# Attention scores on Trainium2: one head in each half of the array's rows, the row maxima added by a second product

## The reference

```
B, S, H, d_k = 4, 1024, 16, 16
Q, K, V = to_heads(split(x @ W_qkv.T)); Q, K = apply_rope(Q), apply_rope(K)
scores = einsum('bhqd,bhkd->bhqk', Q, K) / sqrt(d_k)
scores = where(causal, scores, -inf)
attn = softmax(scores, axis=-1)
out = einsum('bhqk,bhkd->bhqd', attn, V)
```

## Time and profile before

| | us |
|---|---|
| median of 3 runs | 1749.88 |
| lowest and highest | 1743.73, 1751.45 |
| profiled execution | 1757.38 |
| its span | 1755.3 |
| PE busy in the span | 1537.1 (88%) |
| DVE busy | 1001.3 (57%) |
| ACT busy | 734.5 (42%) |
| POOL busy | 573.0 (33%) |

### The profile page before, as it was taken

The page is one execution under the profiler, slowest core; times in us unless marked ns, Lnnn a source line. Parts: engine busy times, 40 slices in busy tenths (PEclk is TensorE's granted clock), DMA queues, the critical chain, the costliest instruction groups (busy, mean ns, idle before and its releaser), DMA issues. The chain is left out here.

```text
span 1755.3 us, 31129 instructions
## 1 busy us (share of the span) xinstructions
PE 1537.1 (88%) x9903; PEld 1148.9 (65%) x9903; DVE 1001.3 (57%) x3394; ACT 734.5 (42%) x1537; POOL 573.0 (33%) x1009
## 2 busy tenths in 40 slices
PE   6999999972999999588698999999999577579978
PEld 3677777752999998344375666666665466468857
DVE  3344555441323232488697888888885456445548
ACT  3444444420222222233245777767777222234410
POOL 3123333323000000677433223223223254535520
PEclk9999999985999999799699999999999788689989
DMA  7001111114777775688869667676660555445536
GB/s 218 1 25 49 49 49 49 37 49 141 207 215 214 209 210 156 184 266 266 224 96 202 93 92 116 92 115 92 92 92 32 175 184 164 129 129 157 157 125 209
DMA packets 170062, 235.21 MB, mean 134 GB/s; under 512 B 25040, under 2 KB 121936, under 8 KB 169776
## 3 DMA queue, kind: packets, MB, share of 16 engines
q1 hardware_dynamic: 134128, 171.55, 42.3%
q0 software_dynamic: 13008, 35.57, 6.1%
q10 hardware_dynamic: 22768, 26.11, 4.7%
HBM read 147.90 MB, written 84.98 MB: 133 GB/s over the span
## 5 line engine op out<-in xcount | busy, mean ns | idle before, releaser
L1983 ACT ACTIVATE t_probs<-t_ps_st 128x512 f32<-128x512 f32 x576 | 313.1, 596 | 134.5 <-PE t_ps_st L2037 125.1
L1964 DVE CUSTOM_DVE_ANT_0 t_seen<-t_ps_s,t_later 128x512 bf16<-128x512 f32 (+3 forms) x512 | 285.7, 587 | 23.3 <-PE t_ps_s L2023 21.3
L2037 PE MATMUL t_ps_st<-t_qs,t_ks 128*128 128x512 f32 (+3 forms) x768 | 244.2, 367 | 6.5 <-ACT t_probs L1983 5.4
L2023 PE MATMUL t_ps_s<-t_ks,t_qs 96*128 96x512 f32 (+3 forms) x768 | 249.1, 364 | 0.6 <-ACT t_neg_max L1976 0.5
L1936 POOL TENSOR_SCALAR_AFFINE_SELECT t_probs<-t_probs 128x128 f32<-128x128 f32 x512 | 137.2, 300 | 313.9 <-ACT t_probs L1983 312.2
L2037 PEld LDWEIGHTS t_ps_st<-t_qs,t_ks 128*128 128x128 f32 x768 | 137.7, 190 | 80.6 <-ACT t_probs L1983 43.4
L1964 DVE CUSTOM_DVE_ANT_0 t_seen<-t_ps_s,t_later,t_first_max 128x512 bf16<-128x512 f32 (+3 forms) x256 | 140.6, 549 | 50.9 <-PE t_ps_s L2023 50.7
L1524 POOL DMA_INDIRECT d_ye<-outputs_dram,r_pos_all x64 | 64.2, 1003 | 303.3 <-POOLq L1304 285.5
L2053 PE MATMUL t_ps_o<-t_probs,t_vs 128*17 128x256 f32 (+1 forms) x2560 | 155.7, 362 | 0.5 <-issue 0.5
L2023 PEld LDWEIGHTS t_ps_s<-t_ks,t_qs 96*128 96x128 f32 x768 | 139.6, 191 | 18.4 <-DVE t_first_max L1964 1.8
L1345 PE MATMUL m_ps_h<-m_xt,m_w_t 128*128 128x128 f32 x1136 | 140.9, 278 | 0.0
(11 more groups left out here) (329 smaller groups left out, 2711.1 us busy)
## 6 DMA issues: line engine op xcount, KB each, us to landing
m_w_t<-in_w_dram SPq DMA_DIRECT2D x71, 512.0 KB, 4.1
t_qs<-qkt_dram SPq DMA_DIRECT2D x124, 128.0 KB, 5.8
t_ks<-qkt_dram SPq DMA_DIRECT2D x124, 128.0 KB, 5.6
m_x_t<-gathered_dram SPq DMA_DIRECT2D x79, 128.5 KB
m_x_t<-gathered_dram SPq DMA_DIRECT2D x71, 128.0 KB, 3.8
outputs_dram<-m_y ACTq DMA_DIRECT2D x71, 128.0 KB, 4.0
qkt_dram<-d_hi ACTq DMA_DIRECT2D x32, 256.0 KB
qkt_dram<-d_lo SPq DMA_DIRECT2D x32, 256.0 KB
```

The source lines that it names most:

```text
L1964: nc.vector.tensor_tensor_reduce(out=seen[:, (NP * p + x) % (RS + 1), 0:keys], in0=bank_of(p, x)[:, 0:keys], in1=masks, scale=1.0, scalar= ...
L1983: nc.scalar.activation(probs[:, p % 2, i // NST, base:base + STC], ps_st[(NX * p + i) % RT][:], ACT.Exp, scale=HD ** -0.5).then_inc(exp_re ...
L2023: nc.tensor.matmul(bank_of(p, x)[:, 0:keys], q[0:MAX_ROW, head, qc * P:(qc + 1) * P], k[0:MAX_ROW, head, k0:k0 + keys], start=True, stop=T ...
L2037: last = nc.tensor.matmul(ps_st[(NX * p + i) % RT][:, col:col + width], k[:, head, kc * P:(kc + 1) * P], q[:, head, q0:q0 + width], start= ...
```

## The change

Head 0 of a pair now lies in partitions 0 to 63 and head 1 in 64 to 127 of tiles half as wide (`[P, SEQ]`). The same bytes are loaded, still by eight DMAs a pair; a broadcast in the source repeats the part of k. A score matmul takes the 64 rows of its head (`half`), and pieces alternate between the heads, one bank each.

The maxima have tiles of their own: `maxima` (two, in turn), row 0 for head 0 and row 64 for head 1, the rest zero, and `first_ones`, whose rows 0 and 64 are one and the rest zero. For each turned product there is a second one that adds it to the same bank. Within a chunk the order is: first product of head 0, of head 1, second product of head 0, of head 1. SP writes the maxima by two DMAs in place of one.

A step is now twice as long: 9 a pair, with the same chunk of both heads, two or four pieces, and averages at steps 0, 2, 4, 5 and 7. `LAG` is 14 of these steps. The transpose stays in step 2, while the chunks of the earlier pair start at step 5, three long steps later; before it was step 9, seven half as long ones later. The negation comes on ACT behind the exponentials of the same step. Three banks for the turned chunks stay. The masks on POOL and the exponentials go by turns through the heads.

```diff
-    rows = hl * 2 * DM + which * DM + (p % PAIRS) * 2 * HD
-    eng.dma_start(dst[part * HD:(part + 1) * HD].bitcast(FP32),
-                  qkt_dram[rows:rows + 2 * HD, bass.ts(p // PAIRS, SEQ)].rearrange("(h d) t -> d h t", h=2)).then_inc(loaded, 16)
+KS = 4 * HD
 
 
 def load_heads(eng, p, q, k, qkt_dram, loaded):
-    for part in range(4):
-        load_head_rows(eng, p, q, 0, part, part % 2, qkt_dram, loaded)
-        load_head_rows(eng, p, k, 1, part, part // 2, qkt_dram, loaded)
+    rows = qkt_dram.rearrange("(l w n d) t -> l w n d t", l=2, w=2, d=HD)
+    cols = bass.ts(p // PAIRS, SEQ)
+    for h in range(2):
+        head = (p % PAIRS) * 2 + h
+        for part in range(2):
+            half = slice(h * KS + 2 * part * HD, h * KS + 2 * (part + 1) * HD)
+            eng.dma_start(q[half].bitcast(FP32), rows[:, 0, head, :, cols]).then_inc(loaded, 16)
+            eng.dma_start(k[half].bitcast(FP32), rows[part:part + 1, 1, head, :, cols].broadcast_to([2, HD, SEQ])).then_inc(loaded, 16)
...
-    MAX_ROW = 96
     RT, RS = 3, 4
-    ks = [k_first] + [sb(f"t_ks{i}", [P, 2, SEQ], FP32R) for i in range(1, RINGQ)]
-    qs = [q_first] + [sb(f"t_qs{i}", [P, 2, SEQ], FP32R) for i in range(1, RINGQ)]
+    ks = [k_first] + [sb(f"t_ks{i}", [P, SEQ], FP32R) for i in range(1, RINGQ)]
+    qs = [q_first] + [sb(f"t_qs{i}", [P, SEQ], FP32R) for i in range(1, RINGQ)]
+    maxima = [sb(f"t_maxima{i}", [P, SEQ], FP32R) for i in range(2)]
+    first_ones = sb("t_first_ones", [P, P], FP32R)
...
-    units = [[u for i in range(NC) for u in ((0, NC - 1 - i), (1, i))], [u for i in range(NC) for u in ((0, i), (1, NC - 1 - i))]]
+    wides = [[NC - 1 - i for i in range(HALF)], [HALF + i for i in range(HALF)]]
     row_pieces = []
-    for each in units:
+    for each in wides:
         mine = []
-        for a, b in zip(each[0::2], each[1::2]):
-            (wh, wq), (nh, nq) = (a, b) if a[1] >= HALF else (b, a)
-            mine += [(wh, wq, 0, STC), (nh, nq, 0, (nq + 1) * P), (wh, wq, STC, (wq + 1) * P - STC)]
+        for wide in each:
+            narrow = NC - 1 - wide
+            for qc, k0, keys in ((wide, 0, STC), (narrow, 0, (narrow + 1) * P), (wide, STC, (wide + 1) * P - STC)):
+                mine += [(head, qc, k0, keys) for head in range(2)]
...
-    upto = [(i + 1) * NP // NX for i in range(NX)]
-    avg_at = {1: (0, 1), 5: (2, 3), 9: (4, 5), 12: (6, 7), 16: (8, 9)}
-    LAG = 27
-    LAST = LAG + (pairs + 1) * NX
+    upto = [2 * ((i + 1) * NP // 2 // NST) for i in range(NST)]
+    avg_at = {0: (0, 1), 2: (2, 3), 4: (4, 5), 5: (6, 7), 7: (8, 9)}
+    LAG = 14
+    LAST = LAG + (pairs + 1) * NST
...
     for p in range(pairs + 1):
-        for i in range(NX):
+        for i in range(NST):
...
             def row(p):
-                s = p % RINGQ
-                if p < RINGQ:
-                    sp.wait_ge(rows_filled, 2 * p + 1)
+                if p == 0:
+                    sp.wait_ge(rows_filled, 5)
+                wait(sp, st_done, NX * (p - 1))
                 sp.wait_ge(neg_ready, p + 1)
-                sp.dma_start(qs[s][MAX_ROW:MAX_ROW + 1].bitcast(FP32).rearrange("o h (c q) -> o (h c) q", c=NC),
-                             neg_max[:, p % 2, :].bitcast(FP32)).then_inc(row_loaded[s], 16)
+                for h in range(2):
+                    sp.dma_start(maxima[p % 2][h * KS:h * KS + 1].bitcast(FP32).rearrange("o (c q) -> o c q", c=NC),
+                                 neg_max[h * NC:(h + 1) * NC, p % 2, :].bitcast(FP32)).then_inc(row_loaded[p % 2], 16)
...
+            nc.gpsimd.memset(first_ones[:].bitcast(FP32), 0.0).then_inc(rows_filled, 1)
+            for m in maxima:
+                nc.gpsimd.memset(m[:].bitcast(FP32), 0.0).then_inc(rows_filled, 1)
...
+            pool.wait_ge(rows_filled, 3)
+            for h in range(2):
+                nc.gpsimd.memset(first_ones[h * KS:h * KS + 1].bitcast(FP32), 1.0).then_inc(rows_filled, 1)
+                pool.wait_ge(rows_filled, 4 + h)
...
-                        dve.wait_ge(piece_ready, NP * p + x - 1)
+                        dve.wait_ge(piece_ready, NP * p + x - 3)
...
             for step in range(LAST):
-                p, i = divmod(step, NX)
-                q, j = divmod(step - LAG, NX)
-                if step == 4 * NX:
+                p, i = divmod(step, NST)
+                q, j = divmod(step - LAG, NST)
+                if step == 4 * NST:
                     fetch(act)
                 if live(q):
-                    exponentials(q, j)
-                if i == 3 and live(p - 1):
+                    exponentials(q, 2 * j)
+                    exponentials(q, 2 * j + 1)
+                if i == TURN and live(p - 1):
                     negate(p - 1)
-                if j == NX - 2 and live(q - 1):
+                if j == NST - 1 and live(q - 1):
                     take_out(q - 1)
...
@@ -2017,10 +2017,9 @@
                 q, k = qs[p % RINGQ], ks[p % RINGQ]
                 if x == 0:
                     pe.wait_ge(qk_loaded[p % RINGQ], 128 * (p // RINGQ + 1))
...
                 bank_free(p, x)
-                nc.tensor.matmul(bank_of(p, x)[:, 0:keys], q[0:MAX_ROW, head, qc * P:(qc + 1) * P], k[0:MAX_ROW, head, k0:k0 + keys],
+                half = slice(head * KS, (head + 1) * KS)
+                nc.tensor.matmul(bank_of(p, x)[:, 0:keys], q[half, qc * P:(qc + 1) * P], k[half, k0:k0 + keys],
                                  start=True, stop=True).then_inc(s_done, 1)
...
-            def chunk(p, i):
-                q, k, head = qs[p % RINGQ], ks[p % RINGQ], i // NST
-                if i == 0:
-                    pe.wait_ge(row_loaded[p % RINGQ], 16 * (p // RINGQ + 1))
-                wait(pe, exp_ready, NX * p + i - RT + 1)
-                for kc, q0, col, width in chunks[i % NST]:
-                    last = nc.tensor.matmul(ps_st[(NX * p + i) % RT][:, col:col + width], k[:, head, kc * P:(kc + 1) * P], q[:, head, q0:q0 + width],
-                                            start=True, stop=True)
-                last.then_inc(st_done, 1)
+            def chunk(p, n):
+                q, k = qs[p % RINGQ], ks[p % RINGQ]
+                if n == 0:
+                    pe.wait_ge(row_loaded[p % 2], 32 * (p // 2 + 1))
+                for kc, q0, col, width in chunks[n]:
+                    for head in range(2):
+                        at, half = NX * p + 2 * n + head, slice(head * KS, (head + 1) * KS)
+                        if col == 0:
+                            wait(pe, exp_ready, at - RT + 1)
+                        nc.tensor.matmul(ps_st[at % RT][:, col:col + width], k[half, kc * P:(kc + 1) * P], q[half, q0:q0 + width],
+                                         start=True, stop=False, skip_group_check=True)
+                    for head in range(2):
+                        at, half = NX * p + 2 * n + head, slice(head * KS, (head + 1) * KS)
+                        last = nc.tensor.matmul(ps_st[at % RT][:, col:col + width], first_ones[half], maxima[p % 2][half, q0:q0 + width],
+                                                start=False, stop=True, skip_group_check=True)
+                        if col + width == STC:
+                            last.then_inc(st_done, 1)
...
             for step in range(LAST):
-                p, i = divmod(step, NX)
-                q, j = divmod(step - LAG, NX)
+                p, i = divmod(step, NST)
+                q, j = divmod(step - LAG, NST)
                 if live(q):
                     chunk(q, j)
                 elif step < LAG:
-                    keep_busy(i, 2 * P)
+                    keep_busy(2 * i, 2 * P)
+                    keep_busy(2 * i + 1, 2 * P)
```

More of the change, by code:

```diff
@@ L1754, in attention @@
     VR = HD + 1
-    KS = 4 * HD
     STC = 4 * P
@@ L1826, in attention @@
     rows_filled, later_zeroed, ones_filled = sem("t_rows_filled"), sem("t_later_zeroed"), sem("t_ones_filled")
+    row_loaded = [sem(f"t_row_loaded{s}") for s in range(2)]
     filled, set_up = sem("t_filled"), sem("t_set_up")
     qk_loaded = [first_loaded] + [sem(f"t_qk_loaded{s}") for s in range(1, RINGQ)]
-    row_loaded = [sem(f"t_row_loaded{s}") for s in range(RINGQ)]
     stored = [sem(f"t_stored{s}") for s in range(2)]
@@ L1916, in _ @@
             pool.wait_ge(set_up, 1)
-            for p in range(1, RINGQ):
-                zero_rows(p)
-                nc.gpsimd.memset(ks[p][KS:P].bitcast(FP32), 1.0).then_inc(rows_filled, 1)
-            pool.wait_ge(rows_filled, 2 * RINGQ - 1)
+            pool.wait_ge(rows_filled, 3)
+            for h in range(2):
+                nc.gpsimd.memset(first_ones[h * KS:h * KS + 1].bitcast(FP32), 1.0).then_inc(rows_filled, 1)
+                pool.wait_ge(rows_filled, 4 + h)
             nc.gpsimd.memset(vs[:], 1.0).then_inc(ones_filled, 1)
@@ L1931, in mask @@
             def mask(p):
-                for head in range(2):
-                    for kc, n, at in diagonals:
-                        pool.wait_ge(exp_ready, NX * p + NST * head + n + 1)
```

(9 more changed lines are left out.)

17 lines of the change are left out of this document (5 added, 12 removed).

## The result

The changed kernel takes 2006.4 us (2005.5 to 2007.8 in four runs), the kernel before beside it 1750.7: a ratio of 1.147 [1.144, 1.150]. I had forecast 1738 us and a range to 1785, so it is 256 us slower where I expected 12 faster. The profiled execution spans 2004.6 us. One execution of all that follow, a fourth of e1_spread at 8108 us, is in the slow state and is left out.

The account below looks back on a forecast made before the run. PE was taken to bound attention. Its work fell 2.25 us a pair to 11.95, but new waits left a period of 14.05 against 14.47: 13 us off, less 1.5 for late maxima, giving 1738 us, range 1712 to 1785.

Parts of the forecast that it names:

- The loads of q and k: DMA loads for attention: eight of 128 KB as before, issued three pairs ahead, so they cost nothing.
- The overlap: PE's score and turned products: two heads' 64-row halves stream at once, taking scores from 4.5 to 2.25 us a pair.
- A (halves queue): PE's matmuls: 64-row halves run one after another, 19.0 us a pair, 140 us more, 1890; chance 0.08.
- B (weight loads queue): PE: matmuls overlap but weight loads queue, two at 0.11 a step; 15.3 us a pair, 27 more, 1777; chance 0.14.
- The maxima's chain: From transpose to chunk 0, through exponentials, negation and two DMAs: 3.75 us, a PE wait of 1.1 us a pair.
- the wait for the negation: Fourth score matmul after the transpose reuses its bank and waits for ACT, about 0.8 us, hidden beneath the DMA.
- The stretch from chunk 0 to the transpose: PE's rest of a pair: chunks, scores, four averages and waits of 0.77 us, summing to 10.05 us.
- The loop through ACT: Head 1's turned product waits for the previous chunk's exponential: 1.15 us, giving waits of 0.48 and 0.29 us.
- After 6 and 8 other waits cover it: Turned chunks following chunks 6 and 8: waits for ACT's exponential add nothing there.
- A block of averages: PE's averages: two rounds cost 0.99 us and 0.09 on the way in; with the short fifth, 5.0 a pair.
- rival C: Score pieces wait for DVE's banks: 0.3 to 0.8 us more a pair, a wash at 1747 to 1763; chance 0.2.
- Rival D: Waits are shorter and DVE becomes the bound at 12.8 us a pair: 52 us less, 1698; chance 0.08.

Follow-up runs that it names:

- e1_spread: The changed kernel with the q and k loads reading a head's 16 rows as outer dimension again, all else kept: 1806 us, 1.033 of before.
- e2: The kernel before with only the changed kernel's loads of q and k, outer dimension 2 in the source: 1994.0 us, 1.137 of before.
- e7: The changed kernel with e1_spread's loads, transpose and negation first, averages in eight blocks, no second product, 49 rows a head: 1730.0 us, 0.988 of before.
- e4: e1_spread with PE's transpose ahead of its step's chunk and ACT's negation ahead of that step's exponentials: 1792.1 us, 1.023 of before.
- e5: e1_spread with the averages in eight blocks, six of them of one round, instead of five blocks: 1793.1 us, 1.023 of before.

## Why the prediction was wrong

**The failing step** is the sentence "The loads of q and k: eight DMAs of 128 KB as before, issued three pairs ahead: nothing." I had compared their number, their size and their lead, and not their outermost dimension, which the diff changes from 16 to 2. Its price is 242 us (e2), of which 31 x 7.4 = 229 lie between the transposes. It is a cost of rate, so a lead of three pairs does not hide it. It shows at the maxima's DMA, which is issued behind loads and needed at once; but the period is set by 1 MB a pair at some 47 GB/s. That PE would otherwise have waited for q and k themselves is my reading; no run took the maxima's DMA out of that queue.

**The overlap holds**, as forecast, so rivals A (halves queue) and B (weight loads queue) fall: products of two heads start 3 to 20 ns apart, their weight loads too, and the next two follow 0.24 us later at 512 columns, 0.18 at 384 and 0.06 at 128 (1137.54 to 1137.60 in e1), which is less than my floor of 0.11.

**The maxima's chain** of 3.75 us measured 3.96, in the shape forecast: the wait for the negation 0.81 (forecast 0.8), and the waits of PE's weight loads for the landing 8.9 us in all of e1's stage (forecast 0.2 a pair and 1.5, so 7.7). The 0.2 is SP: it takes 1.40 us for both issues, so the second comes 0.70 behind the first and not 0.47.

**The stretch from chunk 0 to the transpose**, forecast at 10.05, was 11.57 and 12.44, and this made e1 54 us slower than before and not 12 faster. Three terms were mis-sized. The loop through ACT is 1.42 for 1.15, at two places, because the first product's step was left out of it: 0.5 us a pair. "After 6 and 8 other waits cover it" is wrong after 8: chunk 0's head 1 starts 0.52 and 0.62 us behind head 0 (1126.24, 1141.77), waiting for the exponential of chunk 8. A block of averages costs 0.1 more than my sum had, at the first product behind it: 0.2 for the two of this stretch whose product is not in a loop already. Together 1.3 us, and with the 0.25 that the sum had not placed this is what the first pair took more. Every second pair takes 0.9 us more (16.4 against 15.5), and two waits for DVE's banks stand in it, 0.27 and 0.37 us (at 1143.19 and 1150.19): rival C's mechanism, which I had given 0.2, beside my own. Rival D (DVE the bound) was no rival for this kernel; e7 comes near it, where 13.2 us a pair stand beside the 12.8 worked out for it.

Even without the loads, then, the forecast would have had the sign wrong: 1.033 [1.023, 1.044]. What I had weighed most, the halves' streaming, was right; what decided lay, beside the loads, in waits of 0.3 to 0.9 us that I summed one by one.

## What to carry to other kernels

Of a DMA that a change rewrites, compare the outermost dimension of source and destination before and after, not only bytes and number; in the profile, a DMA share that falls while the wait for a small DMA rises is the sign. Work taken from a bounding engine is worth something only once the waits behind it are gone: list the buffers that the change makes scarcer and close the loop through each engine that frees them (here e4 and e5, worth 0.5 us a pair each alone and 1.5 together). Where the saved work leaves PE with idle or thin stretches, read the granted clock of the changed kernel first.
